# Second attention: the values' products of a pair of heads in four blocks instead of eight

## The chip, the cores and the metric

The kernel runs on one core of a Trainium2 chip. The metric is the device time of one execution, in microseconds. Engines are named as in the profile: PE (TensorE, matrix products), PEld (its weight loads), DVE (VectorE), ACT (ScalarE), POOL (GpSimd), SP (the queue that issues DMAs).

## The reference, cut to what matters

The kernel computes two transformer layers over 2 batches of 1024 tokens of 128 features. The change is in the attention of the second layer, with 16 heads of 64 features:

```python
scores = jnp.einsum('bknh,bqnh->bnqk', keys, queries) / jnp.sqrt(jnp.asarray(H, scores_dtype(residual)))
causal_mask = q_idx < k_idx
scores = jnp.where(causal_mask[None, None, :, :], jnp.asarray(EPS, scores.dtype), scores)
probs = jax.nn.softmax(scores, axis=3)
weighted = jnp.einsum('bnqk,bknh->bqnh', probs, values)
out = jnp.einsum('bqnh,nhe->bqe', weighted, W_output) + Bias_output
```

Masked scores are set to 1e-10 and not to minus infinity, so masked keys keep a weight in the softmax, and their values enter the sum as well.

## The kernel before, in words

Each engine has its own program, in the order in which it is written, and semaphores tie them together. There is no planner: the order of TensorE's products around the change is written out by hand in `pair(p)` (line 1014).

A batch has 8 pairs of heads. The 1024 keys are 8 tiles of 128; scores stand with keys on partitions and queries on columns, so tile t has the columns from t x 128 on. The scores of a tile and a head (`scores(p, t, h)`, L966 and L969) go to the PSUM banks of head h; ScalarE takes their exponents (L1586) into a tile of `EE` or, for tiles 5 and 7, `att_in`; VectorE copies the masked keys' weight under the diagonal (`diagonal`, a predicated copy, L2077) and so raises the semaphore `diag`. Then the values of that tile can be multiplied (`values(p, t)`, L986), which accumulate in banks 6 and 7 for both heads, each head in its own half of TensorE's columns (64 wide), over the 8 tiles. `values_masked(p)` (L999) adds what the masked keys of later tiles give. The denominators are sums over keys: GpSimd adds the exponents of all tiles into `Esum` (L2454, L2463), and TensorE multiplies them by ones (`denominators`, L1010) into banks 6 and 7, after the values there have been copied out. ScalarE inverts them by a logarithm and an exponential (L1603, L1605). GpSimd multiplies pair p - 1 by the inverse (`normalise`, L2433), between tiles 3 and 4 of pair p.

While pair p is worked on, the maxima of pair p + 1 are made in 24 units (`maxima`, L926 and L929, 128 to 512 columns each): TensorE writes a unit to bank 4 or 5, VectorE reduces it (L2052), and unit x may start only when unit x - 2 is reduced. After the last unit VectorE takes the top (L2059, L2061, tile `mx`), TensorE transposes it (`turn_maxima`, L938), and VectorE (L2067, L2068) and ScalarE (L1616, L1617) write it as a row under the next pair's queries, for which the first scores of that pair wait. The projections of pair p + 2 (`project_qk`, L901 and L904) and of the next group's values (`project_v`, L912) stand between the units; ScalarE writes their high parts (L1547 to L1561), VectorE their low parts (L2027, L2040). The second half of a pair's high and low parts is made at the beginning of the pair before it: the first maxima wait for these low parts (line 1035).

Waits that the prediction's steps touch: scores of tile t wait for the exponent of tile t - 1 of the same head (line 957); `values(p, 0)` waits for the logarithm of the earlier pair's denominators (line 980); the turn waits for `m_top` (line 935); GpSimd's chain of a pair waits for the denominators of the pair before (line 2450); `exponents(p, t, 0)` waits for the values of tile t of the pair before (line 1582), since they read the same tile.

Of the kernel before, what the change touches and what calls it, by code (L numbers as in the profile page):

```python
# [19 lines left out]
NT = T // P  # L20
# [46 lines left out]
def layer_program(nc, A, out, sorted_in, sorted_out, weight_rows):  # L67
    ctx = ExitStack()
    with ctx:
# [561 lines left out]
        def _(pe):  # L631
# [253 lines left out]
            def attention1(b):  # L885
# [55 lines left out]
                def mask_row(p, h):  # L941

                    n = n0 + p
                    if h == 1:
                        pe.wait_ge(s["p2_exp"], 2 * NT * n + 1)
                    elif p >= 1:
                        pe.wait_ge(s["p2_exp"], 2 * NT * n)
                    for half in range(2):
                        mm = pe.matmul(banks(2 - 2 * h + half, BANK), row_pick[0:HD + 1, :],
                                       M2[h][p % 2][0:HD + 1, half * BANK:(half + 1) * BANK], start=True, stop=True)  # L950
                    mm.then_inc(s["f_ps"], 1)
# [62 lines left out]
                def pair(p):  # L1014

                    n = n0 + p
                    prev, follows, second = p >= 1, p < PAIRS - 1, p < PAIRS - 2

                    def next_maxima(first, end):

                        if follows:
                            maxima(p + 1, first, end)

                    pe.wait_ge(s["m_row_a"], n + 1)
                    pe.wait_ge(s["m_row_b"], n + 1)
                    scores(p, 0, 0)
                    if prev:
                        values(p - 1, 5)
                    mask_row(p, 0)
                    if prev:  # L1030
                        values(p - 1, 6)
                        values(p - 1, 7)
                    mask_row(p, 1)
                    if follows:
                        pe.wait_ge(s["lo_out"], 8 * (n + 1) + 8)
                    next_maxima(0, 3)
                    scores(p, 0, 1)
                    next_maxima(3, 4)
                    scores(p, 1, 0)
                    next_maxima(4, 5)  # L1040
                    scores(p, 1, 1)
                    if prev:
                        denominators(p - 1)
                    next_maxima(5, 6)
                    scores(p, 2, 0)
                    next_maxima(6, 7)
                    scores(p, 2, 1)
                    next_maxima(7, 8)
                    scores(p, 3, 0)
                    next_maxima(8, 9)  # L1050
                    scores(p, 3, 1)
                    next_maxima(9, 10)
                    values(p, 0)
                    next_maxima(10, 11)
                    scores(p, 4, 0)
                    next_maxima(11, 12)
                    scores(p, 4, 1)
                    if second:
                        pe.wait_ge(s["p2_exp"], 2 * NT * n + NT)
                        project_v(p // 2 + 1, p % 2, (0, 1))  # L1060
                    next_maxima(12, 13)
                    if second:
                        project_v(p // 2 + 1, p % 2, (2, 3))
                    next_maxima(13, 14)
                    values(p, 1)
                    next_maxima(14, 15)
                    scores(p, 5, 0)
                    next_maxima(15, 16)
                    scores(p, 5, 1)
                    next_maxima(16, 17)  # L1070
                    if second:
                        pe.wait_ge(s["v_out"], 1 + 2 * (g0 + 1) + p + 1)
                        project_qk(p + 2, 0, "k")
                    next_maxima(17, 18)
                    if second:
                        project_qk(p + 2, 0, "q")
                    next_maxima(18, 19)
                    values(p, 2)
                    next_maxima(19, 20)
                    values_masked(p)  # L1080
                    next_maxima(20, 21)
                    scores(p, 6, 0)
                    next_maxima(21, 22)
                    scores(p, 6, 1)
                    next_maxima(22, NU)
                    values(p, 3)
                    scores(p, 7, 0)
                    scores(p, 7, 1)
                    if follows:
                        if second:  # L1090
                            pe.wait_ge(s["lo_out"], 8 * (n + 2) + 4)
                        else:
                            pe.wait_ge(s["p2_exp"], 2 * NT * n + NT)
                        turn_maxima(p + 1)
                    if second:
                        pe.wait_ge(s["mx_red"], (n + 2) * NU)
                        project_qk(p + 2, 1)
                    values(p, 4)

                pe.wait_ge(hT_low, 3 * b + 2)  # L1100
# [14 lines left out]
                for p in range(PAIRS):  # L1115
                    pair(p)
# [1468 lines left out]
```

## Time and profile before

| what | us |
|---|---|
| time, median of 3 runs | 2212.29 |
| lowest and highest of them | 2203.16, 2216.28 |
| span of the profiled execution, first to last instruction | 2208.8 |
| PE busy in it | 1973.9 (89%) |
| DVE busy | 1437.3 (65%) |
| ACT busy | 981.3 (44%) |
| POOL busy | 585.7 (27%) |

The profiled execution's own time is known by its span alone; what lies around it isn't measured for that execution. The turns of the second attention stand at 705 to 975 us of the span in the first batch and 1791 to 2059 us in the second. The busy shares are averages over stages with different limits, so the stretch of the change has to be read by itself.

### The profile page before, as it was taken

Reading aid. Unit: us, or ns where it says so; the run is one execution under the profiler, and the core shown is the slowest. Engines: PE = TensorE matmul, PEld = TensorE weight load, DVE = VectorE, ACT = ScalarE, POOL = GpSimd, SP = SyncE. Lnnn points to the kernel's source line nnn. Section 1 sums busy time; section 2 is a strip of 40 time slices with the busy share of each in tenths; the row PEclk is TensorE's granted clock in tenths of the full one; section 3 lists DMA queues with packets and bytes.
Section 4 is the critical chain, followed back from the end, with each engine's and each line's share of the span. In section 5 each row is a group of like instructions: output and inputs, shape, how many; then the busy total and the mean of one; then the engine's idle time right before and its main releaser. Section 6 shows DMA issues by size and latency. Waiting matters only on the chain.

```text
span 2208.8 us, 32078 instructions
## 1 busy us (share of the span) xinstructions
PE 1973.9 (89%) x10106; PEld 1173.6 (53%) x10106; DVE 1437.3 (65%) x2492; ACT 981.3 (44%) x1377; POOL 585.7 (27%) x549
## 2 busy tenths in 40 slices
PE   6899999996997999998888999999979889999985
PEld 4444444443784555556644444444448755555554
DVE  7677788865327777753467877778561377777343
ACT  2445454441224666662334444444413256656422
POOL 0000000000101798884120000000010047897821
PEclk7999999998887999998879999999979879999987
DMA  2366665578000000000516566656760000000024
GB/s 94 84 154 160 155 147 139 141 160 236 27 1 10 3 9 6 1 1 30 162 39 153 142 145 142 144 141 152 180 199 1 1 10 11 1 6 1 1 81 134
DMA packets 84847, 188.01 MB, mean 85 GB/s; under 512 B 17697, under 2 KB 46754, under 8 KB 83106
## 3 DMA queue, kind: packets, MB, share of 16 engines
q1 hardware_dynamic: 83650, 183.76, 32.9%
q0 software_dynamic: 1024, 2.10, 0.3%
q8 instruction: 89, 1.46, 0.3%
q14 instruction: 84, 0.69, 0.1%
HBM read 178.47 MB, written 8.91 MB: 85 GB/s over the span
## 4 chain that ended last, share of the span: by engine, by line
PE 67%; DVE 14%; issue 9%; ACT 3%; DMA 3%; POOL 3%; SPq 1%; DVEq 0%; another core or an unknown queue 0%; POOLq 0%; ACTq 0%
PE PS L814 10%; PE PS L786 5%; PE PS L750 5%; PE PS L986 4%; PE PS L926 4%; PE PS L966 3%; DVE mx L1919 3%; PE PS L881 3%; PE PS L1159 3%; PE PS L969 3%; PE PS L771 3%; PE PS L776 3%; PE PS L1218 2%; DMA V<-weight_rows 2%; POOL Esum L2463 2%
## 5 line engine op out<-in xcount | busy, mean ns | idle before, releaser
L1919 DVE TENSOR_REDUCE mx<-PS 128x8 f32<-128x512 f32 x512 | 329.5, 685 | 178.7 <-PE PS L750 163.9
L2463 POOL TENSOR_TENSOR Esum<-Esum,EE 128x512 f32<-128x512 f32 (+3 forms) x320 | 340.2, 1092 | 15.2 <-POOL Esum L2463 10.7
L1948 DVE TENSOR_TENSOR EE<-EE,V 128x1024 f32<-128x1024 f32 x256 | 303.0, 1218 | 46.2 <-DMA V<-weight_rows 45.8
L1502 ACT ACTIVATE EE<-PS 128x1024 f32<-128x1024 f32 x256 | 260.1, 1025 | 142.5 <-PE PS L776 140.5
L2052 DVE TENSOR_REDUCE mrow<-PS 128x1 f32<-128x512 f32 (+3 forms) x384 | 204.8, 552 | 98.5 <-PE PS L929 70.3
L2405 POOL TENSOR_TENSOR QA<-hT,QA 128x512 fp32r<-128x512 f32 x2 | 2.6, 1284 | 996.8 <-ACT hT L1690 996.8
L814 PE MATMUL PS<-EE,Vlater 128*64 128x512 f32 x1024 | 250.7, 609 | 9.4 <-ACT U L1468 8.3
L750 PE MATMUL PS<-KA,QA 128*128 128x512 f32 x512 | 204.1, 454 | 31.9 <-DVE mx L1919 25.9
L1586 ACT ACTIVATE EE<-PS 128x1024 f32<-128x1024 f32 (+2 forms) x192 | 138.2, 740 | 120.2 <-PE PS L969 118.1
L771 PE MATMUL PS<-QA,KA 128*128 128x512 f32 x512 | 185.1, 443 | 0.0
L750 PEld LDWEIGHTS PS<-KA,QA 128*128 128x128 f32 x512 | 97.8, 196 | 130.5 <-DVE mx L1919 88.5
L776 PE MATMUL PS<-QB,KB 80*128 80x512 f32 x512 | 163.1, 400 | 0.0
L986 PE MATMUL PS<-EE,V 128*64 128x512 f32 (+3 forms) x640 | 131.2, 522 | 0.0
L814 PEld LDWEIGHTS PS<-EE,Vlater 128*64 128x64 f32 x1024 | 61.8, 136 | 115.6 <-issue 91.9
L2077 DVE COPY_PREDICATED EE<-consts,F 128x256 f32<-128x256 int32 x96 | 89.1, 928 | 50.4 <-ACT EE L1586 50.3
L786 PE MATMUL PS<-EE,consts 128*32 128x512 f32 x1024 | 116.5, 595 | 0.8 <-DVE QA L1896 0.8
L771 PEld LDWEIGHTS PS<-QA,KA 128*128 128x128 f32 x512 | 91.8, 192 | 42.6 <-issue 26.8
L776 PEld LDWEIGHTS PS<-QB,KB 80*128 80x128 f32 x512 | 98.1, 192 | 22.3
L926 PE MATMUL PS<-KA,QA 128*128 128x512 f32 (+1 forms) x192 | 89.2, 465 | 19.9 <-DVE mrow L2052 12.8
L2454 POOL TENSOR_TENSOR Esum<-F,consts 128x1024 f32<-128x1024 f32 x32 | 62.2, 1966 | 95.0 <-PE PS L1010 63.7
L926 PE MATMUL PS<-KC,QC 128*128 128x512 f32 (+1 forms) x192 | 84.7, 441 | 0.5
L2445 POOL TENSOR_TENSOR Vlater<-V 128x256 f32<-128x256 f32 x8 | 5.8, 721 | 269.2 <-DVE V L2088 269.2
(321 smaller groups left out, 3386.1 us busy)
## 6 DMA issues: line engine op xcount, KB each, us to landing
V<-weight_rows SPq DMA_DIRECT2D x512, 256.0 KB, 5.5
EE<-in_w SPq DMA_DIRECT2D x48, 192.0 KB, 2.7
V<-in_Wg SPq DMA_DIRECT2D x4, 1024.0 KB, 6.4
EE<-in_Wu SPq DMA_DIRECT2D x4, 1024.0 KB, 11.4
EE<-in_Wd SPq DMA_DIRECT2D x4, 1024.0 KB, 13.2
sorted_out<-U SPq DMA_DIRECT2D x12, 256.0 KB, 3.3
wo<-in_wo SPq DMA_DIRECT2D x5, 512.0 KB, 4.4
wq_s<-in_wq SPq DMA_DIRECT2D x17, 128.0 KB, 3.0
```

The source lines that it names most:

```text
L750: pe.matmul(banks(5 + x % 2, BANK), Q_HIGH[u][:, t * P:(t + 1) * P], KA[g % 2][:, half * BANK:(half + 1) * BANK], start=True, stop=True).t ...
L771: pe.matmul(banks(own, hi - lo, lo), KA[g % 2][:, t * P:(t + 1) * P], Q_HIGH[u][:, lo:hi], start=True, stop=False)
L776: mm = pe.matmul(banks(own, hi - lo, lo), KB[g % 2][0:krows, t * P:(t + 1) * P], Q_LOW[u][0:krows, lo:hi], start=False, stop=True)
L786: mm = pe.matmul(PS[32 * j:32 * j + 32, 4 * BANK:5 * BANK], chunk_sum[:, a, :], EE[i % 2][:, 2 * a + odd, half * BANK:(half + 1) * BANK], ...
L814: mm = pe.matmul(PS[HD * half:HD * half + HD, 7 * BANK:8 * BANK], V0[i // GH % 2][:, t, :], EE[i % 2][:, t, half * BANK:(half + 1) * BANK] ...
L926: mm = pe.matmul(banks(4 + h, hi - lo), M1[h][p % 2][:, t * P:(t + 1) * P], S1[h][p % 2][:, lo:hi], start=True, stop=not own)
L986: mm = pe.matmul(PS[HD * h:HD * h + HD, 6 * BANK + lo:6 * BANK + hi], V1[g % 2][:, t, at:at + HD], e_tile(t)[:, h, lo - t * P:hi - t * P], ...
L1502: act.activation(EE[i % 2][:, t, :], banks(2 * (t % 2)), ACT.Exp, scale=QSCALE).then_inc(s["p2_exp"], 1)
L1919: dve.tensor_reduce(mx[:, t, half * 8:half * 8 + 8], banks(5 + x % 2, BANK).rearrange("p (c k) -> p c k", c=8), AX, ALU.max).then_inc(s["p ...
L1948: dve.tensor_tensor(EE[i % 2][:, t, :], EE[i % 2][:, t, :], weight_ring[a % 2][:, odd, :], ALU.mult).then_inc(p3_mul, 1)
L2052: dve.tensor_reduce(mrow1[:, h, t, half:half + 1], banks(4 + h, width), AX, ALU.max).then_inc(s["mx_red"], 1)
L2463: ins = pool.tensor_tensor(Esum[:, h, lo:hi], Esum[:, h, lo:hi], e_tile(t)[:, h, lo - t * P:hi - t * P], ALU.add)
```

## The change

Only the order of calls in TensorE's `pair(p)` changes. Before, a pair's values are multiplied in eight blocks, with other work between them: tile 4 of the pair before, then tile 5, tiles 6 and 7, and of the pair itself tile 0, tile 1, tile 2, the masked keys, tile 3. After it there are four: tiles 5 to 7 of the pair before behind the first masked row; tiles 0 and 1 where tile 1 was; tile 2 and the masked keys; tiles 3 and 4 behind the turned maxima and the late projection, where tile 4 was. No instruction and no wait is added or removed.

```diff
@@ -1024,12 +1024,10 @@
                     scores(p, 0, 0)
-                    if prev:
-                        values(p - 1, 5)
                     mask_row(p, 0)
                     if prev:
-                        values(p - 1, 6)
-                        values(p - 1, 7)
+                        for t in range(5, NT):
+                            values(p - 1, t)
                     mask_row(p, 1)
@@ -1049,9 +1047,7 @@
                     scores(p, 3, 1)
-                    next_maxima(9, 10)
-                    values(p, 0)
-                    next_maxima(10, 11)
+                    next_maxima(9, 11)
                     scores(p, 4, 0)
@@ -1062,6 +1058,7 @@
                     next_maxima(13, 14)
+                    values(p, 0)
                     values(p, 1)
                     next_maxima(14, 15)
@@ -1074,16 +1071,14 @@
-                    next_maxima(18, 19)
+                    next_maxima(18, 20)
                     values(p, 2)
-                    next_maxima(19, 20)
                     values_masked(p)
                     next_maxima(20, 21)
@@
                     next_maxima(22, NU)
-                    values(p, 3)
                     scores(p, 7, 0)
                     scores(p, 7, 1)
@@ -1095,6 +1090,7 @@
                         project_qk(p + 2, 1)
+                    values(p, 3)
                     values(p, 4)
```

## Rows read from the trace of the kernel before

**Rows 1.** The page, busy us, share of the span and instructions of each engine.

```profile
PE 1973.9 (89%) x10106; PEld 1173.6 (53%) x10106; DVE 1437.3 (65%) x2492; ACT 981.3 (44%) x1377; POOL 585.7 (27%) x549
```

**Rows 2.** Busy time by stretches: stretch, length, each engine's busy us, granted clock, DMA.

```profile
783.97:822.99 39.02, 37.15 (x200) 21.33 (x201) 29.08 (x48) 24.84 (x35) 35.40 (x35) 1.00 0.03 8
822.99:862.01 39.02, 37.16 (x201) 21.35 (x202) 29.07 (x48) 24.83 (x35) 30.84 (x29) 1.00 0.03 8
```

**Rows 3.** Timeline, PE, one pair: start, length, operation, count, idle time before and releaser.

```profile
783.97 1.03 PE L938 MATMUL PS<-consts,mx 128*33 128x128 f32 x8 [1.14 <-issue]
...
786.65 1.08 PE L986 MATMUL PS<-EE,V 128*64 128x512 f32 x4
787.66 0.73 PE L966 MATMUL PS<-QA,KA 128*128 128x512 f32 x2
...
792.02 0.33 PE L926 MATMUL PS<-KA,QA 128*128 128x128 f32 x1 [0.25 <-DVE QD L2040]
...
796.38 1.94 PE L1010 MATMUL PS<-Esum,ones_cols 128*64 128x512 f32 x8
...
802.46 0.39 PE L926 MATMUL PS<-KC,QC 128*128 128x512 f32 x1
802.78 1.94 PE L986 MATMUL PS<-EE,V 128*64 128x512 f32 x8
804.65 0.33 PE L926 MATMUL PS<-KA,QA 128*128 128x128 f32 x1
...
804.86 0.48 PE L966 MATMUL PS<-QA,KA 128*128 128x512 f32 x1
...
810.00 0.38 PE L926 MATMUL PS<-KA,QA 128*128 128x256 f32 x1
...
819.96 1.30 PE L986 MATMUL PS<-EE,V 128*64 128x128 f32 x8
821.18 0.33 PE L966 MATMUL PS<-QA,KA 128*128 128x128 f32 x1
...
822.99 1.03 PE L938 MATMUL PS<-consts,mx 128*33 128x128 f32 x8 [1.15 <-issue]
```

**Rows 4.** Timeline, DVE: mx in the first pair, then reductions, copy, mx.

```profile
744.56 0.19 DVE L2061 TENSOR_TENSOR mx<-mtop,consts 128x16 f32<-128x16 f32 x1
...
802.73 1.27 DVE L2052 TENSOR_REDUCE mrow<-PS 128x1 f32<-128x512 f32 x2
...
813.94 0.56 DVE L2052 TENSOR_REDUCE mrow<-PS 128x1 f32<-128x384 f32 x1 [0.38 <-PE PS L929]
...
819.32 1.20 DVE L2077 COPY_PREDICATED EE<-consts,F 128x256 f32<-128x256 int32 x1
...
821.96 0.94 DVE L2061 TENSOR_TENSOR mx<-mtop,consts 128x16 f32<-128x16 f32 x1
```

**Rows 5.** Timeline, POOL: start of a pair's sums, normalisation, tile 4.

```profile
798.59 3.94 POOL L2454 TENSOR_TENSOR Esum<-F,consts 128x1024 f32<-128x1024 f32 x2 [2.11 <-PE PS L1010]
...
820.17 1.46 POOL L2433 TENSOR_TENSOR U<-U,xn 128x512 f32<-128x512 f32 x1
821.59 1.26 POOL L2433 TENSOR_TENSOR U<-U,xn 128x512 f32<-128x512 f32 x1
822.81 2.48 POOL L2463 TENSOR_TENSOR Esum<-Esum,EE 128x512 f32<-128x512 f32 x2
```

**Rows 6.** Timeline, ACT: exponents of tile 3, both heads.

```profile
803.33 1.28 ACT L1586 ACTIVATE EE<-PS 128x640 f32<-128x640 f32 x2
```

**Rows 7.** Timeline, PE: sixth and seventh denominators, the seventh in both batches.

```profile
952.43 1.94 PE L1010 MATMUL PS<-Esum,ones_cols 128*64 128x512 f32 x8
...
986.37 1.94 PE L1010 MATMUL PS<-Esum,ones_cols 128*64 128x512 f32 x8 [1.61 <-POOL Esum L2463]
...
2070.45 3.36 PE L1010 MATMUL PS<-Esum,ones_cols 128*64 128x512 f32 x8 [1.62 <-POOL Esum L2463]
```

**Rows 8.** Waits of PE: who waited for whom, us in total, times, longest.

```profile
PE PS L938 <- issue: 14.0, 12, 1.3
```

## The prediction

> **What bounds the kernel now.** The page gives TensorE 89% of the span [rows 1], which invites the reading "TensorE is the bound, every switch saved is time saved". The reader should not stop there. I next read the stretch by stages: inside the second attention two successive pairs of heads, measured from one transposition of the maxima ("turn", L938) to the next, take 39.02 us each, with TensorE busy 37.15 and 37.16 us, at the full granted clock [rows 2]. About 1.9 us per pair are idle, and the equal lengths, to the hundredth, say that something rigid closes a loop.
>
> The timeline of TensorE shows where: each turn stands behind 1.14 or 1.15 us of idle time [rows 3]. The turn waits for the two-input VectorE operation that writes mx (L2061). In the first pair that operation takes 0.19 us; in the steady pair it is started at 821.96 and takes 0.94, ending at 822.90 [rows 4]. GpSimd's operations around it end at 821.6 and about 822.8 [rows 5]: VectorE stood still until GpSimd's current operation ended. The same is seen on the predicated copy of tile 6: started at 819.32, done only after GpSimd's operation ends at 820.17 [rows 4, 5].
>
> The Trainium skill (SBUF — State Buffer, "SBUF: two separate sides") says that VectorE with two SBUF inputs and GpSimd take a shared port pair as an exclusive lock for a whole instruction; these two durations agree.
>
> And GpSimd's own chain is rigid: it starts at 798.59, when the denominators' products have ended (they start at 796.38), and its normalisation's last operation ends at about 822.8 [rows 3, 5]. So the loop is: turn 783.97, to denominators 796.38 (12.41 us of TensorE, VectorE and ScalarE), to GpSimd's start 798.59 (2.21), to the end of its normalisation (24.22), to the next turn 822.99 (0.18). The sum is 39.02. What is saved on TensorE between denominators and turn only lengthens the idle time in front of the turn; what is added between turn and denominators is paid in full.
>
> **The change part by part.** No instruction is added or removed; only TensorE's queue is reordered. A block of values' products costs something fixed: four products of 512 columns (each stands in the trace as two instructions) take 802.78 to 804.65, 1.87 us; two take 786.65 to 787.66, 1.01 [rows 3]; two cost 0.86, so 0.15 is fixed. The maximum in front of a block takes 0.32 (802.46 to 802.78) where 512 columns at 2.4 GHz are 0.21, and the one behind it 0.21 (804.65 to 804.86) where 2 x 128 columns are 0.11 [rows 3]. Together 0.36 us a block, eight blocks a pair before, four after.
>
> The Trainium skill (TensorEngine Tiling, "Key Properties") says that changing the tiling mode drains TensorE; the 0.36 is in line with it, and by that rule alone the change would gain: that is rival 4.
>
> (1) Tile 3's values go behind the turn, in front of the next pair's first scores. They take 1.22 (819.96 to 821.18), less 0.15 since they join tile 4's block: +1.07 for scores of tile 0. Is it covered? Only if those scores were waiting, but they start at 787.66 straight behind tile 4's block, with no idle time [rows 3]. Behind them the first maximum of the next pair (792.02) waits 0.25 for VectorE's low query part [rows 3], which comes by a chain from these scores (exponent, high part, low part): it moves with them. Denominators: +1.07. Lower bound 0.8, if the 0.25 were given back; upper 1.5, as in even pairs VectorE's copies meet GpSimd's sums of V.
>
> (2) Tile 5's values join 6 and 7 behind the first masked row. It saves up to 0.36 in front of that 0.25 wait: 0, bounds -0.3 and 0.
>
> (3) Tile 0's values leave the place between units 9 and 10. They covered two waits there. Unit 10 needs VectorE's reduction of unit 8, which runs from 802.73 for 0.64 [rows 4]; unit 10 would start at 803.4 instead of 802.8. Scores of tile 4 need ScalarE's exponent of tile 3: started at 803.33, 0.70 long with its tail (half of the 1.28 row plus 0.06), so 804.03; with 0.05 for the signal 804.08, against 804.86 [rows 3, 6]: only 0.78 earlier, though 1.87 us were taken out. The products come back in front of tile 1's at 1.87 - 0.15 = 1.72. Net at unit 14 (810.00): -0.78 + 1.72 = +0.94. Bounds +0.7 and +1.1 from 0.1 us uncertainty on each of the two waits.
>
> (4) Tile 2's values join the masked ones: about -0.36 on TensorE, 0 at the turn, since from 813.94 on VectorE works without a gap (reduction, low keys and queries, reductions, copy of tile 6) [rows 4].
>
> (5) What the +0.94 does to the turn. VectorE's chain from 813.94 starts with a reduction of a unit that TensorE delivers, so it moves by 0.94, and the copy of tile 6 is asked for at 819.32 + 0.94 = 820.26. GpSimd's operation ends at 820.17 [rows 5]. Before, the copy was 0.85 us early for that end; now it misses it by 0.09 and stands until the next, about 821.4 (1.24 later, half of the row 822.81 of 2.48 [rows 5]). The two last reductions and the top follow as before (mx is asked for 1.79 after 820.17), so at about 823.2, and GpSimd's operation that then runs ends at 822.8 + 1.24 = 824.05: the turn comes at 824.24, +1.25. If the copy catches 820.17 instead, mx is asked for in time for 822.8 and this term is 0. Upper bound of the term 2.5, a second operation missed.
>
> Steady interval: 1.07 + 1.25 = +2.32. Denominators start at 796.38 and, four intervals on, at 952.43 [rows 3, 7]: 156.05, or 4 x 39.01. With the interval before 796.38 these are five in each of two batches: 10 x 2.32 = 23.2.
>
> First interval of a batch: no normalisation runs then, mx is free (0.19); item 1 costs 1.07 and item 3 an estimated 0.5, 1.6 x 2 = 3.2. End of a batch, pairs 6 and 7: without projections nothing hides item 3. The seventh denominators waited 1.61 for GpSimd [rows 7], which absorbs that much. I put pair 6 at 1.07 + about 3 of later turn less 1.6, and the last pair at 1.87 - 0.3 that no longer covers ScalarE's inverse: about 4 a batch, bounds 1 and 5. 2 x 4 = 8.
>
> Sum: 23.2 + 3.2 + 8 = 34.4. Against the profiled execution's span of 2208.8 that is 2243.2. The profiled run's time around its span isn't shown; the median of the runs, 2212.29, lies 3.5 above the span, and the runs spread from 2203.16 to 2216.28, so I add 3.5: **2246.7**, rounded to 2247.
>
> **The rivals.** (1) The copy catches its gap. Same loop, but item 5 is 0. For it: the miss is 0.09 us by a sum with errors of that size. 10 x 1.07 + 3.2 + 2 x 4 = 22, of which the end may give back 2: 2233.
>
> (2) The clock falls as well. In the forecast TensorE stands about 2.6 us in front of each turn (scores of tile 7 end near 821.6, turn at 824.24). In the first batch a wait of 1.61 is followed by eight products in 1.94; in the second batch the same 1.62 is followed by the same eight in 3.36, the clock at its lower level of 1.2 GHz [rows 7]. Twelve waits of turns, together 14.0 and 1.3 at most, stand in the trace [rows 8], and over the two shown the clock stayed at 1.00 [rows 2]. A fall behind each steady turn costs 1.4 to 1.9: 10 x 1.65 = +16 on the forecast: 2263. Against it: one case of two, and the phase is not mine to tell.
>
> The Trainium skill (TensorE: Matmul & The Clock Gate, "What's actually happening") says that idleness takes the clock to half and activity releases it; the 3.36 agrees.
>
> (3) The turn catches the earlier end. If TensorE delivered so much sooner that mx were asked for before 821.6 rather than at 821.96, the loop would lose 1.22 and gain 1.07: no change, 2212. It needs VectorE's chain 0.4 earlier, where I have it 0.94 later.
>
> (4) Faster, TensorE being the bound. 4 blocks x 16 pairs x 0.36 = 23 us: 2189. It decides if the denominators don't come later than now, that is if tile 3's 1.07 disappears in a wait for the turned maxima's rows. Against it: no idle time stands before the scores at 787.66 [rows 3], and 1.14 stands before the turn, where tile 3's cover is taken away.
>
> **How the numbers follow.** Forecast 0.42, rival 1 0.20, rival 2 0.16, rival 3 0.13, rival 4 0.09. A change of 0.5%, 11 us, is about what a measurement of this kernel can tell. Slower: 0.42 + 0.20 + 0.16 = 0.78; same 0.13; faster 0.09. The forecast's own range, with 1.0 to 1.5 for item 1 and the bounds of the ends, is 2238 to 2256. The range of 8 in 10 reaches from below rival 1 to rival 2: 2219 to 2266.
>
> **What would show it.** Right: intervals from turn to turn of about 41.3 instead of 39.02, idle time in front of turns of about 2.6, denominators about 13.5 behind the turn instead of 12.41; the copy of tile 6 (L2077) over 1.4 long; idle time in front of units 10 to 12 and scores of tile 4 that is not there now; mx (L2061) ending with a GpSimd operation of tile 4. Intervals of 40.1 are rival 1; a granted clock under 1.00 over the steady intervals rival 2; 39.0 rival 3. Wrong altogether: intervals below 38.8, with denominators no more than 12.4 behind the turn.

## The result, and the profile after

The changed kernel takes 2248.14 us (median of four runs, 2244.65 to 2251.87), the kernel before 2209.81 (four runs, 2203.16 to 2216.28): a ratio of 1.018 [1.0159, 1.0201], 38.3 us slower. Forecast were 2247 and "slower" at 0.78. The total hides errors that cancel; they are told below. Each kernel left one profile, so what is said of its intervals, and of how often the clock fell in them, is one execution's; that of the changed kernel was the fastest of its four.

The page's busy times of the changed kernel, as in [rows 1]:

```profile
PE 1972.2 (88%) x10106; PEld 1180.5 (53%) x10106; DVE 1444.1 (64%) x2492; ACT 979.2 (44%) x1377; POOL 580.5 (26%) x549
```

TensorE has lost 1.7 us of work and the kernel has gained 38 us of time. Whoever reads only this view sees an improvement.

The timeline of TensorE over the second and third pair (start, length, operation, count, idle time before and its releaser), to be laid beside [rows 3]:

```profile
783.95 1.03 PE L938 MATMUL PS<-consts,mx 128*33 128x128 f32 x8 [2.28 <-issue]
...
786.63 2.15 PE L986 MATMUL PS<-EE,V 128*64 128x128 f32 x12
788.72 0.73 PE L966 MATMUL PS<-QA,KA 128*128 128x512 f32 x2
...
792.96 0.33 PE L926 MATMUL PS<-KA,QA 128*128 128x128 f32 x1 [0.48 <-DVE QD L2036]
...
797.29 1.94 PE L1010 MATMUL PS<-Esum,ones_cols 128*64 128x512 f32 x8
...
804.38 0.33 PE L926 MATMUL PS<-KA,QA 128*128 128x128 f32 x1 [0.62 <-DVE mrow L2048]
...
804.98 0.50 PE L966 MATMUL PS<-QA,KA 128*128 128x512 f32 x1 [0.21 <-ACT EE L1582]
...
811.87 0.39 PE L926 MATMUL PS<-KA,QA 128*128 128x256 f32 x1
...
816.40 0.44 PE L926 MATMUL PS<-KC,QC 128*128 128x384 f32 x1 [0.63 <-DVE mrow L2048]
...
825.07 1.03 PE L938 MATMUL PS<-consts,mx 128*33 128x128 f32 x8 [2.28 <-issue]
```

The turns stand at almost the same place (783.95, before 783.97), so the two timelines can be read as one clock. What the reader is to see: the block behind the turn is longer (2.15 instead of 1.08) and everything behind it is later, the scores at 788.72 instead of 787.66 and the denominators at 797.29 instead of 796.38. At 804.38 and 804.98 stand two waits, 0.62 and 0.21, that tile 0's products had covered. Unit 14 comes at 811.87 instead of 810.00. A third wait, 0.63 in front of 816.40, I had not foreseen. The next turn is at 825.07 instead of 822.99, behind 2.28 of idle time instead of 1.15.

VectorE's timeline of the same stretch, to be laid beside [rows 4]:

```profile
814.22 1.55 DVE L2073 COPY_PREDICATED att_in<-consts,F 128x256 f32<-128x256 int32 x1
...
818.40 0.56 DVE L2048 TENSOR_REDUCE mrow<-PS 128x1 f32<-128x384 f32 x1
...
821.63 0.98 DVE L2073 COPY_PREDICATED EE<-consts,F 128x256 f32<-128x256 int32 x1
...
824.04 0.93 DVE L2057 TENSOR_TENSOR mx<-mtop,consts 128x16 f32<-128x16 f32 x1
```

Two of them as they stood in the kernel before, the copy of tile 5 and the reduction behind the low parts of the keys:

```profile
812.35 0.64 DVE L2077 COPY_PREDICATED att_in<-consts,F 128x256 f32<-128x256 int32 x1
...
816.09 0.56 DVE L2052 TENSOR_REDUCE mrow<-PS 128x1 f32<-128x384 f32 x1
```

And GpSimd's, to be laid beside [rows 5]:

```profile
799.51 3.93 POOL L2450 TENSOR_TENSOR Esum<-F,consts 128x1024 f32<-128x1024 f32 x2 [4.36 <-PE PS L1010]
...
821.03 2.68 POOL L2429 TENSOR_TENSOR U<-U,xn 128x512 f32<-128x512 f32 x2
823.67 2.48 POOL L2459 TENSOR_TENSOR Esum<-Esum,EE 128x512 f32<-128x512 f32 x2
```

GpSimd starts 0.92 later, with the denominators. The copy of tile 5 is asked for at 814.22 and lasts 1.55; the same copy took 0.64 before. mx is asked for at 824.04, when the first of two GpSimd additions (823.67, about 1.24 long) is already running, and is written as that one ends, at about 824.95. Counted from GpSimd's start, it is asked for at 24.53, before at 23.37, and so gets the end of the operation after the one that it got before.

Last, two intervals from turn to denominators (stretch, length, busy us of the five engines, granted clock, DMA share, GB/s):

```profile
825.07:838.43 13.36, 12.69 (x66) 7.35 (x66) 7.97 (x15) 9.03 (x12) 5.54 (x7) 1.00 0.01 2
907.32:922.31 14.99, 14.31 (x67) 7.93 (x67) 7.80 (x15) 9.02 (x12) 5.54 (x7) 0.89 0.00 0
```

The same work takes 13.36 at a granted clock of 1.00 and 14.99 at 0.89: in or behind the wait of 2.28 the clock went for a while to its lower level (1.2 GHz). This is so in seven of the ten steady intervals. The waits view, beside [rows 8]:

```profile
PE PS L938 <- issue: 31.0, 16, 2.3
```

Where the 34.0 us of span went (2208.8 to 2242.8), for the two batches together. "First intervals" run from the first turn to the first denominators, "steady" from the first denominators to the sixth, "ends" from the sixth to the eighth and last:

| part | predicted | measured |
|---|---|---|
| steady intervals, ten, order of the work | +23.2 | +21.1 |
| steady intervals, clock | 0 (rival 2: +16) | +11.0 |
| first intervals, two | +3.2 | +3.25 (0.33 and 2.92) |
| ends of the two batches, order of the work | +8 | about +6.0 |
| ends of the two batches, clock | 0 | about -3.3 |
| stages that the change doesn't touch | 0 | -4.1 |
| span | +34.4 | +34.0 |

How the ends are parted: together they are 2.75 longer (2.98 and -0.23). The way from the seventh denominators to the last took 36.04 and 37.65 before, at a granted clock of 0.95 and 0.91. The same order of work took 34.39 at a clock of 1.00 in a kernel below (mx without the shared port, second batch), and the changed order 36.28 and 36.27 at 1.00. So the order costs 1.9 a batch there, and 1.1 in front of it (35.06 instead of 33.91 from the sixth to the seventh denominators in the second batch, at 1.00 in both). The rest is the clock, which fell more often at the ends before than after.

### The profile page after: what moved, and what is told of

The parts are those of the page before. It is cut to its first block, busy times and chain, and to the rows that moved or that the text cites. A ratio compares the mean times of both kernels' runs of the same rounds, so it can differ in the third digit from the quotient of the medians.

```text
span 2242.8 us, 32078 instructions
## 1 busy us (share of the span) xinstructions
PE 1972.2 (88%) x10106; PEld 1180.5 (53%) x10106; DVE 1444.1 (64%) x2492; ACT 979.2 (44%) x1377; POOL 580.5 (26%) x549
## 4 chain that ended last, share of the span: by engine, by line
PE 64%; DVE 15%; issue 11%; ACT 4%; DMA 3%; POOL 2%; SPq 1%; DVEq 0%; ACTq 0%; POOLq 0%
PE PS L814 9%; PE PS L786 5%; PE PS L750 5%; PE PS L986 5%; DVE mx L1915 3%; PE PS L926 3%; PE PS L771 3%; PE PS L966 3%; PE PS L1155 3%; PE PS L776 3%; PE PS L881 2%; PE PS L969 2%; PE PS L1214 2%; DMA V<-weight_rows 2%; DVE mrow L2048 2%
## 5 line engine op out<-in xcount | busy, mean ns | idle before, releaser
L750 PEld LDWEIGHTS PS<-KA,QA 128*128 128x128 f32 x512 | 97.3, 195 | 126.9 <-DVE mx L1915 82.5
L986 PE MATMUL PS<-EE,V 128*64 128x512 f32 (+3 forms) x640 | 125.7, 523 | 0.0
L926 PEld LDWEIGHTS PS<-KA,QA 128*128 128x128 f32 x192 | 38.2, 199 | 76.5 <-DVE mrow L2048 41.5
```

The costliest lines, as they stand in the source:

```text
L750: pe.matmul(banks(5 + x % 2, BANK), Q_HIGH[u][:, t * P:(t + 1) * P], KA[g % 2][:, half * BANK:(half + 1) * BANK], start=True, stop=True).t ...
L926: mm = pe.matmul(banks(4 + h, hi - lo), M1[h][p % 2][:, t * P:(t + 1) * P], S1[h][p % 2][:, lo:hi], start=True, stop=not own)
L986: mm = pe.matmul(PS[HD * h:HD * h + HD, 6 * BANK + lo:6 * BANK + hi], V1[g % 2][:, t, at:at + HD], e_tile(t)[:, h, lo - t * P:hi - t * P], ...
```

## The experiments

All medians are of kernels run beside the kernel before on the same chip, which had 2211.18, 2209.66 or 2207.51 there. The steady intervals are told from turn to turn: 39.02 before, 41.12 after where the clock held.

### Each part of the change alone

**Tile 3 alone behind the turn**, on the kernel before:

```
                     next_maxima(22, NU)
-                    values(p, 3)
                     scores(p, 7, 0)
 ...
                         project_qk(p + 2, 1)
+                    values(p, 3)
                     values(p, 4)
```

> The kernel before with one edit: the values of tile 3 stand behind the turned maxima and the late projection, in front of tile 4's. Theory (a loop closed by GpSimd's rigid chain; what stands between turn and denominators is paid, what stands between denominators and turn is not): turn to denominators 13.34 instead of 12.41 (+0.93, as in the changed kernel), denominators to turn unchanged at 26.6, so intervals of 39.95; idle time in front of the turn 2.4 instead of 1.14. 10 intervals x 0.93 + 2 to 3 us at the ends of the batches: +12 us where the clock holds. If the clock falls behind such waits as in the changed kernel (turn to denominators 15.0), up to +13 us more. Rival (TensorE is the bound and only the blocks count): one block less a pair, 16 x 0.36, 6 us faster, intervals of 38.7.

Measured: 2240.8, ratio 1.0143 [1.0123, 1.0163], 30 us more. Its windows of one steady interval, and the turn that begins it:

```profile
784.26:800.52 16.26, 15.94 (x66) 8.50 (x67) 7.79 (x15) 9.13 (x12) 11.32 (x14) 0.81 0.06 17
```

```profile
784.26 1.89 PE L938 MATMUL PS<-consts,mx 128*33 128x128 f32 x8 [2.49 <-issue]
```

The way from denominators to turn is unchanged (26.58 to 26.60, before 26.61). The way from turn to denominators is 13.36 the one time that the clock held, in the first pair of the first batch, where it was 12.30 before: 1.06 for item 1 there. In all ten steady intervals it is 15.0 to 16.8, so the steady price of the order isn't seen alone here; with the 0.95 that the changed kernel shows it is 9.5 us of the ten. In the profiled execution the ten are 32.1 longer, which leaves 22.6 to the clock, more than the 13 that I had allowed, since an interval loses 1.7 to 3.4 by it here and not 1.65.

**Tile 0 alone in front of tile 1:**

```
-                    next_maxima(9, 10)
-                    values(p, 0)
-                    next_maxima(10, 11)
+                    next_maxima(9, 11)
 ...
                     next_maxima(13, 14)
+                    values(p, 0)
                     values(p, 1)
```

> The kernel before with one edit: the values of tile 0 stand in front of tile 1's. Theory (the tile's 1.87 us covered two waits there; moved, they come late enough that VectorE's predicated copies of tiles 5 and 6 miss the ends of GpSimd operations): denominators to turn 27.8 instead of 26.6, turn to denominators unchanged at 12.4, intervals of 40.2, idle time in front of the turn still near 1.1, and no fall of the clock: 10 x 1.17 + about 4 at the ends, +14 to +16 us. Rival (the whole loss is tile 3's): 0, or 6 us faster by the block saved.

Measured: 2231.76, ratio 1.0096 [1.008, 1.0113], 20.6 more. Its turn, and in a second fence the VectorE operations ahead of it:

```profile
826.27 1.03 PE L938 MATMUL PS<-consts,mx 128*33 128x128 f32 x8 [0.92 <-issue]
...
838.53 1.94 PE L1010 MATMUL PS<-Esum,ones_cols 128*64 128x512 f32 x8
```

```profile
815.39 1.57 DVE L2076 COPY_PREDICATED att_in<-consts,F 128x256 f32<-128x256 int32 x1
...
822.82 0.98 DVE L2076 COPY_PREDICATED EE<-consts,F 128x256 f32<-128x256 int32 x1
...
825.22 0.94 DVE L2060 TENSOR_TENSOR mx<-mtop,consts 128x16 f32<-128x16 f32 x1
```

Here the other half of the loop has grown, from denominators to turn 27.80 (+1.19), with turn to denominators at 12.26 to 12.41 and no fall of the clock in the steady intervals: the wait before the turn is only 0.92. The three durations 1.57, 0.98 and 0.94 are those of the changed kernel (1.55, 0.98, 0.93), so the whole change's new waits on VectorE come from tile 0's move. Steady intervals give 11, as expected; the first intervals 2.6 and the ends 7, where I had allowed 4 together. Of the 2.6 some 1.5 is the clock in the second batch's first pair (granted 0.87, before 0.91).

**The merges alone** (tiles 5 to 7 in one block, tile 2 with the masked ones; tiles 0 and 3 stay):

```
                     scores(p, 0, 0)
-                    if prev:
-                        values(p - 1, 5)
                     mask_row(p, 0)
                     if prev:
-                        values(p - 1, 6)
-                        values(p - 1, 7)
+                        for t in range(5, NT):
+                            values(p - 1, t)
 ...
-                    next_maxima(18, 19)
+                    next_maxima(18, 20)
                     values(p, 2)
-                    next_maxima(19, 20)
                     values_masked(p)
```

> The kernel before with two edits: tiles 5 to 7 of the pair before in one block, tile 2 joined to the masked keys; tiles 0 and 3 stay. Theory: both savings end in waits that are there anyway (the 0.25 us in front of the first maximum, VectorE's chain in front of the turn): intervals 39.0, idle time in front of the turn 1.1 to 1.3, time within 3 us of before. Rival (blocks cost on the path): two blocks x 16 x 0.36, 11 us faster.

Measured: 2211.31 (11 runs), ratio 1.0004 [0.999, 1.0017]; intervals 38.97 to 39.02, idle time before the turn 1.12 to 1.16. So two of the four saved blocks cost nothing and bring nothing. The two whose move costs are those of tiles 0 and 3.

### The loop itself

**mx without the shared port.** The operation that writes mx takes two inputs; a third column of constants lets the one-input reduction write mx directly, here on the kernel before:

```
-        mrow1 = sb("mrow1", [P, 2, NT, 2])
+        mrow1 = sb("mrow1", [P, 2, NT, 3])
 ...
-                    dve.tensor_reduce(mtop1[:, :, :], mrow1[:, :, :, :], AX, ALU.max).then_inc(s["m_both"], 1)
-                    dve.wait_ge(s["m_both"], n + 1)
-                    dve.tensor_tensor(mx1..., mtop1[:, :, :], const("eps_row")..., ALU.max)
+                    dve.tensor_reduce(mx1[:, :, 0:33:32]..., mrow1[:, :, :, :], AX, ALU.max)
 ...
+            dve.tensor_copy(mrow1[:, :, :, 2], const("eps_row")...)
```

> The kernel before, order of TensorE unchanged; the last step of the maxima doesn't read two operands from SBUF any more: the constant of its maximum stands as a third column in the tile of maxima, so one reduction writes mx directly, and the two-operand operation is gone. Theory (the turn waits for that operation, which stands until GpSimd's current operation ends): the reduction ends near 25.5 us behind the denominators' start, TensorE reaches the turn at 25.5 as well, so denominators to turn 25.7 instead of 26.6, intervals of 38.1, 12 x 0.9, 11 us faster. Rival (the turn waits for something else, the low parts or a plain reduction): no change.

Measured: 2232.15, ratio 1.0097 [1.0075, 1.012]: 21 slower where I expected 11 faster. Half of the expectation came: denominators to turn is 25.65 where the clock held, and the turn waits 0.17. Its turn and first unit, the copy of tile 7, and two windows:

```profile
782.96 1.03 PE L938 MATMUL PS<-consts,mx 128*33 128x128 f32 x8 [0.17 <-issue]
...
791.84 0.33 PE L926 MATMUL PS<-KA,QA 128*128 128x128 f32 x1 [1.07 <-DVE QD L2040]
```

```profile
787.40 1.27 DVE L2075 COPY_PREDICATED att_in<-consts,F 128x256 f32<-128x256 int32 x1
```

```profile
790.00:792.00 2.00, 0.93 (x5) 0.46 (x3) 1.74 (x3) 1.87 (x2) 1.84 (x4) 1.00 0.00 0
792.00:796.00 4.00, 3.80 (x15) 2.94 (x16) 1.34 (x4) 1.06 (x2) 3.61 (x6) 0.62 0.02 4
```

The turn has come earlier, but GpSimd has not: VectorE's operations behind the turn now meet its sums (the copy of tile 7 lasts 1.27, before 0.45), and the first unit waits 1.07 for them, where it waited 0.25 [rows 3]. Behind that wait the clock fell (0.62 in the next 4 us), and turn to denominators takes 14.8 to 16.1 instead of 12.4 in nine of the ten steady intervals. In the tenth, where the granted clock stayed at 1.00, it takes 13.23, and the whole interval 38.89 against 39.02 before. So the wait had only been moved, which alone is worth a tenth of a microsecond, and the loss is the clock's.

**The same on the changed kernel:**

> The changed kernel, and the last step of the maxima reads no second operand from SBUF (as in the run before, on the kernel before). Theory as it stands now: the lock in front of the turn accounts for 0.9 to 1.0 of the 27.78 us from denominators to turn, so 26.8; but the same lock then meets the operations behind the turn (copy of tile 7, copies of the queries' high part), as that run showed, so the first maximum comes only about 0.2 earlier and turn to denominators grows from 13.34 to about 14.1. Intervals 40.9 to 41.1 where the clock holds, about the time of the changed kernel, 2240 to 2255. Rival (the lock costs time only at the turn): intervals of 40.2, 2237.

Measured: 2236.97, ratio 1.0129 [1.0109, 1.0148], 11 less than the changed kernel. Denominators to turn 26.83 as expected; turn to denominators not 14.1 but 13.35 or 13.88, so intervals of 40.2 or 40.7 where the clock held, and not 41: the rival's 40.2 in part of them. The clock fell in four of ten, in or behind an idle time of 1.31 to 1.33 before the turn. Here the edit pays. The copy of tile 7 is longer here too (0.90 to 0.92 where the clock held), but VectorE stands 0.8 behind it anyway, until the scores that item 1 made later let ScalarE go on. Where the interval is the longer one, VectorE's last cast of the queries lasts 0.96 beside GpSimd's sum of V, otherwise 0.42.

**The changed kernel with TensorE kept busy before the turn**, by five products that nobody reads:

```
                     if second:
+                        pe.wait_ge(s["mx_red"], (n + 2) * NU)
+                        for _ in range(5):
+                            pe.matmul(banks(5, BANK), M1[1][(p + 1) % 2][:, T - P:T], S1[1][(p + 1) % 2][:, BANK:T],
+                                      start=True, stop=True)
```

> The changed kernel with work added: in front of each turn TensorE waits for the last reduction and then repeats a maximum's product of 512 columns five times into bank 5, whose content nobody reads; the result is not changed. It fills 1.1 of the 2.28 us in which TensorE stood there. Theory (the extra over the steady intervals of 41.12 is the clock, which fell behind waits of 2.28 and never behind 1.14): denominators to turn 27.8 as before, turn to denominators 13.34 everywhere, no granted clock under 1.00 in the steady stretch; 8 falls of 1.4 to 1.7 less, 11 to 13 us faster than the changed kernel, 2235 to 2238 beside 2210. Rival (the 1.66 has another cause, or added products cost time): no change or slower than the changed kernel, 2248 to 2256.

Measured: 2241.55, ratio 1.0151 [1.0129, 1.0173], 6.6 less than the changed kernel. Its turn with the added products ahead, and the window behind it:

```profile
829.41 1.43 PE L1091 MATMUL PS<-KC,QC 128*128 128x512 f32 x5 [1.06 <-DVE mrow L2052]
830.71 1.03 PE L938 MATMUL PS<-consts,mx 128*33 128x128 f32 x8
```

```profile
830.71:844.06 13.35, 12.68 (x68) 7.36 (x67) 7.94 (x15) 9.03 (x12) 5.53 (x7) 1.00 0.01 2
```

Turn to denominators is 13.35 to 13.37 in nine of ten steady intervals, with the clock at 1.00, against three of ten; the intervals are 41.23. The ten together give back 8.1 of the 11.0; the other 2.9 are one fall that is left and 0.1 us an interval for the products themselves. This is the test of the clock's part: more work on TensorE, the same order, shorter intervals. Outside the steady ten the profiled execution loses again, 5.4 in the first intervals (among them a fall at the turn ahead of the first batch's first denominators, 14.28 between the two) and 1.5 at the ends, so the times of whole executions show it less clearly: the two ratios' intervals, up to 1.0173 here and from 1.0159 for the changed kernel, just overlap. The intervals carry the test, not the median.

### Other orders of the blocks

**Tiles 0 and 1 joined at the earlier place**, between units 9 and 10, with the harmless merges, whose lines are as above:

```
                     values(p, 0)
+                    values(p, 1)
 ...
-                    next_maxima(13, 14)
-                    values(p, 1)
-                    next_maxima(14, 15)
+                    next_maxima(13, 15)
```

> The kernel before with tiles 0 and 1 joined at the earlier place (between units 9 and 10), tiles 5 to 7 joined, tile 2 joined to the masked keys; tile 3 stays in front of the scores of tile 7. Five blocks a pair instead of eight and nothing moved later. Theory (what costs is the place, not the joining, and the loop closed by GpSimd keeps its length): the stalls at unit 10 and scores of tile 4 don't appear, denominators to turn 26.6, intervals 39.0, idle time in front of the turn 1.1 to 1.3, within 3 us of before. Rival (joining blocks gains): 3 x 16 x 0.36, 17 us faster. Rival (joining itself costs, since tile 4's exponents and their copy come 1.5 later): intervals over 39.5, 5 or more us slower.

Measured: 2235.13, ratio 1.0121 [1.0102, 1.014]; the last rival named there was right. Units 15 and 16 wait for VectorE, which is late from copies of tiles 4 and 5 (1.09 and 1.17). Denominators to turn is 27.97 to 28.00 in the four intervals where the clock held, 1.4 more than before, and 29.2 in the six where it fell behind these two waits:

```profile
810.71 0.39 PE L926 MATMUL PS<-KC,QC 128*128 128x256 f32 x1 [0.66 <-DVE mrow L2048]
...
812.24 0.50 PE L926 MATMUL PS<-KA,QA 128*128 128x512 f32 x1 [0.67 <-DVE mrow L2048]
```

```profile
813.00:816.00 3.00, 3.00 (x6) 1.34 (x4) 2.24 (x3) 1.36 (x2) 3.00 (x4) 0.50 0.00 0
```

**Tile 4 too behind the first masked row**, so that the first scores come about 1.0 us sooner:

```
                     scores(p, 0, 0)
-                    if prev:
-                        values(p - 1, 5)
                     mask_row(p, 0)
                     if prev:
-                        values(p - 1, 6)
-                        values(p - 1, 7)
+                        for t in range(4, NT):
+                            values(p - 1, t)
 ...
-                    values(p, 4)
+                    if not follows:
+                        values(p, 4)
```

> The kernel before with tiles 5 to 7 joined behind the first masked row, and tile 4 of the pair before put in front of them instead of in front of the next pair's first scores. The mirror of the changed kernel's edit of tile 3: 1.01 us leave the path from turn to first scores. Theory (turn to denominators is what counts; but the first maximum waits for VectorE's low parts, whose chain of VectorE's own work from the turn allows only 0.2 less): first scores 1.0 earlier, turn to denominators 12.2, intervals 38.8, 10 x 0.2, 2 us faster to none; idle time in front of the first maximum over 1 us, and the clock may fall there. If TensorE alone counted: intervals of 38.0, 10 us faster.

Measured: 2219.12, ratio 1.0046 [1.003, 1.0062], slower by 9.5. Its first unit:

```profile
829.82 0.33 PE L926 MATMUL PS<-KA,QA 128*128 128x128 f32 x1 [0.95 <-DVE QD L2039]
```

Where the clock held, turn to denominators is 12.37 to 12.39: the earlier scores are worth nothing, since VectorE's low parts come as before and the first unit waits 0.95 for them. In half of the intervals the clock fell behind that wait (13.92 to 14.88). So in the steady intervals less work of TensorE ahead of that unit brings nothing, and more is paid. In the first pair, where the unit waits only 0.25, the same move brought 0.59 (11.71 instead of 12.30).

### With GpSimd's sums shortened

Four kernels leave out most of GpSimd's sums, to see what the order costs when that engine is no longer in the way: the kernel before, the changed one, the merges alone and tile 0 alone. In each:

```
-                                                 const("after").unsqueeze(2).to_broadcast([P, NT, P]), ALU.mult)
+                                                 const("first", 0, NT).unsqueeze(2).to_broadcast([P, NT, P]), ALU.mult)
 ...
+                                hi = lo + 1
```

> The kernel before, order of TensorE unchanged, but GpSimd's additions of exponents are cut to one column each (every wait and signal stays), and the weights in the first product of the sum are positive numbers of another constant; so the denominators, and what follows from them, are other numbers than the reference's. GpSimd's chain is short and holds no shared port late in the pair. Theory: the loop is not closed by GpSimd any more; the turn stands directly behind TensorE's own work, denominators to turn 25.3 instead of 26.6, turn to denominators 12.3, intervals of 37.6, 12 to 18 us faster. Rival (GpSimd is not the loop): intervals of 39.0.

> The changed kernel with GpSimd's additions cut to one column in the same way (denominators other numbers than the reference's). It parts the 2.1 us of an interval into what the order costs by itself and what the shared port adds. Theory: turn to denominators 13.3 (tile 3's 0.93 needs no port), denominators to turn 25.9 to 26.2, so intervals of 39.3 where the clock holds: 1.6 over the kernel before with short sums, 0.5 less than the 2.1 with the real sums. Rival (all of tile 0's cost is the port): 25.3 and 38.6, 0.95 over. Rival (the port plays no part): 2.1 over, 39.7.

> The kernel before with short sums on GpSimd (denominators other numbers than the reference's) and the two neutral edits, tiles 5 to 7 in one block and tile 2 joined to the masked keys. Theory (a block saved pays 0.36 only where TensorE is the bound; here it is, between denominators and turn): 0.3 us less than the kernel before with short sums in denominators to turn, nothing in turn to denominators: intervals of 37.3. Rival (a block saved pays nothing): 37.6.

> The kernel before with short sums on GpSimd (denominators other numbers than the reference's) and tile 0's values in front of tile 1's. Theory (the move uncovers the wait for ScalarE's exponent of tile 3 and VectorE's reduction, 0.94, and the port added the rest of the 1.18): denominators to turn 26.2, 0.9 over the kernel before with short sums, turn to denominators the same 12.3. Rival (the whole 1.18 is the port): 25.3, no difference.

| with short sums | median us | turn to denominators | denominators to turn | interval |
|---|---|---|---|---|
| the kernel before | 2190.32 | 12.27, 12.46 | 25.30 | 37.56, 37.77 |
| the changed kernel | 2227.41 | 13.35 | 26.05 | 39.40 |
| merges alone | 2194.62 | as the first | 25.31 | 37.59, 37.78 |
| tile 0 alone | 2206.09 | 12.28, 12.47 | 26.26 | 38.54, 38.74 |

The values are those of intervals in which the clock held; the medians, of three to nine runs, hold its falls too. The kernel before with short sums is at a ratio of 0.9898 [0.9833, 0.9964], the merges at 0.9946 [0.9929, 0.9963], tile 0 alone at 0.999 and the changed kernel at 1.0086 [1.0064, 1.0108]. The loop through GpSimd costs the kernel before 1.2 to 1.5 us an interval: without it no idle time stands before the turn, and the operation that writes mx took 0.19 us at all fourteen turns behind the two batches' first, where it took 0.94 or 0.95 at ten of them with the real sums. The change still costs 1.6 to 1.8 of its 2.10 (39.40 against 37.56 or 37.77). Tile 0's move alone costs 0.95 of its 1.19, and its two uncovered waits are there as in the changed kernel:

```profile
805.21 0.33 PE L926 MATMUL PS<-KA,QA 128*128 128x128 f32 x1 [0.62 <-DVE mrow L2051]
...
805.81 0.50 PE L966 MATMUL PS<-QA,KA 128*128 128x512 f32 x1 [0.21 <-ACT EE L1585]
```

The merges brought nothing even here, where I had expected 0.3 an interval: the last units wait for VectorE, with short sums 0.26 in the old order and 0.55 with the merges, so what the merges save in front of them becomes wait. That expectation was wrong, and with it the last place where a saved block might have shown.

## Why the prediction was right, and where it was not

The loop. It stands as predicted: intervals of 41.12 where the clock held (41.3 predicted), denominators 13.35 behind the turn (13.5), idle time before the turn 2.28 (2.6). Moving the work between turn and denominators changed that half alone (the first experiment), tile 0's move the other half alone (the second), and the merges neither. Rival 4 (blocks are what costs) falls with them: at no place did a block less bring time.

Item 1, tile 3 behind the turn: +1.07 predicted, +0.93 to +0.96 measured in the steady intervals of the changed kernel and +1.05 and +1.10 in its first pairs. The size of the block was right: the scores of tile 0 stand 4.77 behind the turn instead of 3.69, 1.08 later. Nearly all of it is uncovered, as said. The missing 0.12 is given back on the way to the first unit, where VectorE's last cast of the queries took 0.55 beside GpSimd before and takes 0.42 now.

Items 2 and 4: 0 predicted, 0 measured (the merges alone).

Item 3: +0.94 at unit 14 predicted. In the changed kernel unit 14 stands 27.92 behind the turn, before 26.03: 1.89, of which 0.93 are item 1's and 0.96 this one's. Its two waits, too: unit 10 was put at 803.4, the scores of tile 4 at 804.08, and less item 1's shift they came at 803.47 and 804.07. These two numbers came out of [rows 4, 6] alone.

Item 5 was right in size (+1.25 predicted, +1.17 measured) and wrong in its place. I let the chain move by 0.94 and had tile 6's copy miss GpSimd's end by 0.09. The sign that I had named for it, a copy of tile 6 over 1.4 long, didn't come. What missed was already the copy of tile 5: asked for at 814.22, just as GpSimd had begun an addition of 512 columns, it lasted 1.55. VectorE's chain was then 1.4 late instead of 0.94 (its second reduction of 384 columns starts at 818.40, before at 816.09: 2.31 less item 1's 0.93), TensorE got its third wait of 0.63, and tile 6's copy waited an ordinary 0.98. The turn came at the same slot because GpSimd's ends offer no others: 824.16 in the frame of before, 824.24 predicted. So the third item and the fifth don't split at 0.94 and 1.25 - 0.94 as written; with short sums the order makes 0.95 and the port 0.2 of tile 0's cost, and the sum of the steady interval, 2.32 predicted, was 2.10.

The first intervals were right in their sum, 3.25 for 3.2: 2.15 from turn to denominators, which is item 1 twice, and 1.1 ahead of that, item 3 twice. The split into 0.33 and 2.92 is the clock's, which was low in the first pairs of both kernels (granted 0.87 and 0.91 before, 0.91 and 0.87 after).

What I had wrong in the sum are terms that cancel. **The ends of the batches**: 8 predicted, 2.75 measured. The order costs about 6 there, 3 a batch where I had 4. The last pair is about as said (1.9 for 1.6). In pair 6 I had item 1's 1.07 paid beside the later turn, less the wait of 1.61 [rows 7]; the turn came 2.6 later, but from it to the seventh denominators are 9.94, against 11.41 with the 1.61 in it, so of the 1.07 hardly anything was paid. The other 3.3 are the clock: it fell once and twice at the two ends before, of which the 3.36 of [rows 7] is one, and once and not at all after. **The clock in the steady intervals**: rival 2 was given 0.16 as an alternative, at 1.65 a fall in all ten. It came in seven of ten, at 1.36 to 1.65 each, 11.0 together, and the sign that I had named for it, a granted clock under 1.00 there, came with it. It wasn't an alternative to the forecast but a term of it, with a size between none and all. With these terms right the forecast would have been about 40 on the span, and the part outside the stage (-4.1, unexplained; the runs of the kernel before alone spread over 13 us) brings it back to 34. That the total met the forecast within 0.4 is therefore luck; that each interval grew by about 2.1 for the reasons given is not.

Rival 1 (the copy catches, 40.1 an interval) and rival 3 (39.0) are excluded by the 41.12.

The parts alone do not add: 30 and 20 make 50, the change 38. The order's parts do (item 1's 0.95 and tile 0's 1.19 make 2.14, measured 2.10); the clock's doesn't, since it depends on how long TensorE has stood where. In the first experiment it fell at waits of 2.49 in ten of ten, in the changed kernel at waits of 2.28 in seven.

Left open: whether an order exists that gains. None of the eight other kernels that do the whole computation was faster than the kernel before; only with GpSimd's sums shortened were two, the kernel before and the merges. Open too: why a wait of one length is followed by the lower clock in some intervals and not in others.

## What to carry to other kernels

When the intervals between two like places of a loop are equal to the hundredth while the busiest engine has idle time in each, find the engine that closes the loop, and price an edit by which of its halves it stands in, not by the instructions saved. A block of products in an in-order queue is also the cover of the waits behind it: before moving it, ask for each instruction behind it when its input comes. And enter a possible clock fall as a term of the sum with a count, not as a separate case: here it was a third of what the steady intervals lost.

## What the runs showed of the hardware

**The clock falls behind short waits, and not behind each.** With idle times of 1.13 to 1.15 before the turn (the kernel before) the granted clock stayed at 1.00 in all ten steady intervals, with 2.25 to 2.28 (the changed kernel) it fell in seven of ten, with 2.49 (tile 3 alone) in ten of ten. But it fell too with 1.31 to 1.33 and with 0.99 to 1.00 before the turn (the changed kernel with mx free of the port and with short sums, four of ten each), behind 1.07 (mx without the port, nine of ten), 0.95 (tile 4 behind the mask, half of the intervals) and 0.66 with 0.67 (six of ten), which stand among other short waits: the length of the last one alone does not tell. Five products of no use in the wait kept the clock in nine of ten. The Trainium skill ("TensorE: Matmul & The Clock Gate", "What's actually happening") says that the clock gate follows TensorE's activity; the traces agree. The price for an interval with a fall in it was from 1.2 us (tiles 0 and 1 early, 41.5 against 40.25) to 4.6 (mx without the port, 43.50 against 38.89).

**A wait for the port has the length of the other engine's instruction, so it comes in steps.** In the kernel before, VectorE's predicated copies of 256 columns took 0.44 to 0.46 where GpSimd stood, and 0.63 to 1.57 where they were held; those ended 0.30 to 0.32 us behind GpSimd's running operation. The two-input operation on 128x16 took 0.19 free and 0.94 or 0.95 held, and then ended 0.04 behind it. The step shows in the copy of tile 5: asked for at 812.35 before it took 0.64, at 814.22 after it took 1.55. So a shift of VectorE by some tenths can cost nothing or about a microsecond. The Trainium skill ("SBUF — State Buffer", "SBUF: two separate sides") speaks of an exclusive lock held for a whole instruction; the held durations fit it, and with GpSimd's sums shortened the 128x16 operation took 0.19 at all fourteen turns.
